# Two transformer layers on one core: the first group normalised by VectorE, casts dealt out over the groups, and a gather of two rows ahead of the indices

## The reference

```python
xn = _layernorm(x, axis=-1)                      # no scale, no bias, eps 1e-5
x = x + L0_attn(xn, Wq, Wk, Wv, Wo) + L0_ffn(xn, Wg, bg, W1, b1, W2, b2)
xn = _layernorm(x, axis=-1)
x = x + L1_attn(xn, w_qkv, w_proj, b_proj) + L1_ffn(xn, W_r, W_k, W_v, mu_r, mu_k)
# L0_attn: q, k, v = xn @ W.T, 16 heads of 8; rotary turn of q and k; phi = elu + 1;
#          causal linear attention: running sums of k and of k (x) v, num / den; @ Wo.T
# L0_ffn:  gate = softmax(xn @ Wg + bg) over 8 experts, top 2, weights made to sum to 1;
#          each expert: gelu(xn @ W1[e] + b1[e]) @ W2[e] + b2[e]
# L1_attn: the same kind of attention without causality; L1_ffn: r * (relu(k)^2 @ W_v)
```

## Time and profile before

| | |
|---|---|
| median of the runs | 356.3 us |
| the profiled execution | 356.63 us, its span 354.8 us |
| granted TensorE clock over the span | 0.995 |
| busy: TensorE, VectorE, ScalarE, GpSimd | 340.7, 318.8, 272.5, 210.4 us |
| front (to the start of the choice) | 0 to 35.8 us |
| choice, turns, tables | 35.8 to 59.6 us |
| first expert matmul | 64.23 us |
| last gather's transpose | 264.3 us |

### The profile page before, as it was taken

The page is one execution under the profiler, slowest core; times in us unless marked ns, Lnnn a source line. Parts: engine busy times, 40 slices in busy tenths (PEclk is TensorE's granted clock), DMA queues, the critical chain, the costliest instruction groups (busy, mean ns, idle before and its releaser), DMA issues.

```text
span 354.8 us, 9147 instructions
## 1 busy us (share of the span) xinstructions
PE 340.7 (96%) x2498; PEld 297.2 (84%) x2498; DVE 318.8 (90%) x629; ACT 272.5 (77%) x767; POOL 210.4 (59%) x231
## 2 busy tenths in 40 slices
PE   8999968999999999999999999999999899999995
PEld 3788524699999999999999899999998687778885
DVE  3998899799999999999899899998987799998665
ACT  3887957966988888888687878778985987777751
POOL 3899201853343666766676768777877268884110
PEclk9999989999999999999999999999999999999999
DMA  6866295345353545554555644565452002221112
GB/s 190 237 187 188 82 427 188 107 143 140 98 164 113 173 140 161 148 165 128 178 153 147 172 148 145 158 174 150 132 136 76 17 7 54 60 62 30 30 31 59
DMA packets 45520, 46.98 MB, mean 132 GB/s; under 512 B 6928, under 2 KB 33712, under 8 KB 45216
## 3 DMA queue, kind: packets, MB, share of 16 engines
q1 hardware_dynamic: 40288, 36.88, 33.8%
q0 software_dynamic: 4320, 8.86, 9.5%
q10 hardware_dynamic: 864, 0.67, 0.7%
HBM read 32.88 MB, written 13.50 MB: 131 GB/s over the span
## 4 chain that ended last, share of the span: by engine, by line
PE 86%; DVE 7%; ACT 2%; DMA 2%; issue 2%; POOL 0%; DVEq 0%; POOLq 0%
PE banks L546 18%; PE banks L533 18%; PE banks L672 7%; PE banks L673 7%; PE banks L984 3%; PE banks L342 3%; PE banks L311 3%; PE banks L517 3%; PE banks L1013 2%; PE banks L1060 2%; PE banks L1042 2%; PE banks L333 2%; PE banks L1022 2%; PE banks L748 2%; PE banks L994 2%
## 5 line engine op out<-in xcount | busy, mean ns | idle before, releaser
L461 POOL DMA_INDIRECT xg<-xn_rows,slot_tok x71 | 77.9, 1098 | 77.6 <-PE banks L517 41.6
L563 ACT ACTIVATE xT<-banks,b1T 128x128 f32<-128x128 f32 x284 | 81.7, 375 | 18.1 <-PE banks L533 17.8
L478 POOL DMA_INDIRECT qk_exp<-expert_rows,ranki x64 | 74.1, 1158 | 19.1 <-issue 18.8
L546 PE MATMUL banks<-w_sb,xT 128*128 x568 | 79.0, 282 | 0.0
L533 PE MATMUL banks<-xgT,w 128*128 128x128 f32 x568 | 75.4, 276 | 0.1
L546 PEld LDWEIGHTS banks<-w_sb,xT 128*128 128x128 f32 x568 | 69.3, 192 | 0.6
L533 PEld LDWEIGHTS banks<-xgT,w 128*128 128x128 f32 x568 | 69.0, 192 | 0.6 <-issue 0.6
L684 DVE TENSOR_TENSOR cq<-banks,phi 128x360 f32<-128x360 f32 (+1 forms) x96 | 47.3, 548 | 7.1 <-PE banks L673 6.4
L656 DVE TENSOR_TENSOR low<-outer,high 128x1152 fp32r<-128x1152 f32 x32 | 43.5, 1358 | 4.5 <-ACT high L650 4.3
L650 ACT CAST high<-outer 128x1152 fp32r<-128x1152 f32 x32 | 36.9, 1154 | 9.9 <-DVE outer L639 8.6
L693 DVE TENSOR_REDUCE sums<-cq 128x144 f32<-128x1152 f32 x32 | 43.0, 1342 | 0.1
(11 more groups left out here) (206 smaller groups left out, 687.8 us busy)
## 6 DMA issues: line engine op xcount, KB each, us to landing
w<-in_L_ffn_W SPq DMA_DIRECT2D x71, 256.0 KB
expert_rows<-ye SPq DMA_DIRECT2D x71, 64.0 KB
expert_rows<-x_sb SPq DMA_DIRECT2D x2, 2048.0 KB, 9.0
x_sb<-in_L_attn_x SPq DMA_DIRECT2D x8, 256.0 KB, 4.0
xn_rows<-xn SPq DMA_DIRECT2D x8, 256.0 KB, 2.4
w_sb<-in_L_ffn_W SPq DMA_DIRECT2D x8, 256.0 KB, 3.2
out<-outer SPq DMA_DIRECT2D x7, 256.0 KB, 2.4
xg<-xn_rows,slot_tok POOLq DMA_INDIRECT x71
```

What stands on the lines that cost most here:

```text
L461: pool.indirect_dma_start(out=xg[n][:, :], out_offset=None, in_=xn_dram, in_offset=bass.IndirectOffsetOnAxis(ap=slot_tok[:, j:j + 1], axis ...
L478: pool.indirect_dma_start(out=y_moe[:, i, k, :], out_offset=None, in_=y_dram, in_offset=bass.IndirectOffsetOnAxis(ap=ranki[:, 0, k, i:i + ...
L546: last = nc.tensor.matmul(y, hidT[p][:, c, :], w2_sb[:, ds(e * NC + c, 1), :], start=False, stop=(c == NC - 1))
L563: last = nc.scalar.activation(hidT[p][:, c, :], slot_bank(j)[:, c * P:(c + 1) * P], ACT.Gelu_apprx_tanh, bias=b1T[:, ds(e * NC + c, 1)])
```

## The change

VectorE normalises group 0 itself from mean and rstd (`normalise_first`), tile by tile; GpSimd leaves out the last two operations of `deviation` for that group. TensorE transposes group 0 in two halves into two banks (`xT_first`), ScalarE copies them half by half (`xT_first_scalar`), and TensorE starts the values with the first half (`values1_half`). Nearly all warming matmuls around this go. Queries and keys rotate over three banks (4, 5, 3) instead of two, and a half waits for the products three halves back; the counts of the ranks move from bank 3 to bank 1. The load of the second part of the constants moves from ScalarE's queue to SP's, behind x of group 4; the seven casts go to groups 1 to 4, two, two, two and one. The flags of two memsets are merged. On GpSimd a gather of two rows into `y_tok`, which nobody reads, stands between a wait for `turn_key` and a wait for its own landing, ahead of the wait for `idx_ready`.

```diff
     def deviation(pool, layer, g, n):
...
         nc.gpsimd.tensor_tensor(rstd[n][:, :], ve[n][:, :], mhalf[:, :], ALU.pow).then_inc(rstd_part[layer], 1)
+        if layer == 0 and g == 0:
+            return
...
+    def normalise_first(v):
+        v.wait_ge(rstd_part[0], 1)
+        for k in range(GT):
+            nc.vector.tensor_scalar(xn[0][:, k, :], x_sb[:, k, :], mv[0][:, k, 0:1], rstd[0][:, k:k + 1],
+                                    ALU.subtract, ALU.mult).then_inc(xn_ready[0], 1)
...
+    def xT_first(pe):
+        for h in range(2):
+            for t in range(2):
+                pe.wait_ge(xn_ready[0], 2 * h + t + 1)
+                last = nc.tensor.transpose(ps[h][:, t * P:(t + 1) * P], xn[0][:, 2 * h + t, :], ident)
+            last.then_inc(xT_ps, 1)
+            keep_warm(1)
...
+    def qk_bank(g, h):
+        return ps[(4, 5, 3)[(2 * g + h) % 3]]
 
     def queries1_tensor(pe, g, h, p):
-        if g:
-            pe.wait_ge(rope_ready, g * 2 + h - 1)
+        if g * 2 + h >= 3:
+            pe.wait_ge(rope_ready, g * 2 + h - 2)
...
+    def xT_first_scalar(act):
+        for h in range(2):
+            act.wait_ge(xT_ps, h + 1)
+            nc.scalar.copy(xT[0][:, 2 * h:2 * h + 2, :].rearrange("p a b -> p (a b)"), ps[h][:, 0:2 * P]
+                           ).then_inc(xT_ready, 1)
...
-    counts = ps[3][:, 0:NPRE]
+    counts = ps[1][:, 0:NPRE]
...
             sp.wait_ge(wts_in, 16 * 4)
-            for g in range(2, NG):
+            for g in range(2, 5):
+                load_x(g)
+            sp.dma_start(cq[:, 0:NCONST - NKEPT], consts[:, NKEPT:]).then_inc(passing_in, 16)
+            for g in range(5, NG):
                 load_x(g)
...
-            act.dma_start(cq[:, 0:NCONST - NKEPT], consts[:, NKEPT:]).then_inc(passing_in, 16)
...
-            normalise(act, 0, 0)
-            xT_scalar(act, 0, 0)
+            xT_first_scalar(act)
             normalise(act, 0, 1)
             for g in range(NG):
                 for h in range(2):
                     values1_scalar(act, g, h)
+                if g == 1:
+                    act.wait_ge(passing_in, 16)
+                    # 2 casts; 2 more at g == 2, 2 at g == 3, 1 at g == 4 (all 7 stood behind g == 0)
...
             for n in range(NB):
                 pool.wait_ge(xn_saved[n], 16 * (NG // NB))
+            pool.wait_ge(turn_key, 1)
+            pool.indirect_dma_start(out=y_tok[0:2, 0:D], out_offset=None, in_=xn_dram,
+                                    in_offset=bass.IndirectOffsetOnAxis(ap=ranki[0:2, 1, 0, 0:1], axis=0)
+                                    ).then_inc(first_rows, 16)
+            pool.wait_ge(first_rows, 16)
             pool.wait_ge(idx_ready, 1)
...
-            keep_warm(3)
+            keep_warm(2)
+            xT_first(pe)
             pe.wait_ge(wT_ready, 1)
-            keep_warm(7)
-            xT_tensor(pe, 0, 0)
-            keep_warm(4)
             for g in range(NG):
-                values1_tensor(pe, g, g % 2)
-                queries1_tensor(pe, g, 0, g % 2)
+                if g:
+                    values1_tensor(pe, g, g % 2)
+                    queries1_tensor(pe, g, 0, g % 2)
+                else:
+                    values1_half(pe, 0, 0, 0)
+                    queries1_tensor(pe, 0, 0, 0)
+                    values1_half(pe, 0, 1, 0)
...
-            for g in range(5):
+            for g in range(2):
+                loaded_moments(g)
+            normalise_first(v)
+            for g in range(2, 5):
                 loaded_moments(g)
```

More of the change, by code:

```diff
@@ L294, in normalise @@
         n = g % NB
-        act.wait_ge(rstd_ready[layer], g + 1)
+        act.wait_ge(rstd_ready[layer], g + layer)
         if g >= NB:
             if layer == 0:
-                act.wait_ge(xT_ps, g - NB + 1)
+                act.wait_ge(xT_ps, g - NB + 2)
                 act.wait_ge(xn_saved[n], g // NB * 16)
@@ L312, in keep_warm @@
                              start=True, stop=True)
+    def xT_first(pe):
[5 more added lines that the diff above has]
+            keep_warm(1)
     def xT_tensor(pe, g, p):
-        pe.wait_ge(xn_ready[0], g + 1)
-        if from_(g, 2):
-            pe.wait_ge(xT_ready, g - 1)
+        pe.wait_ge(xn_ready[0], g + GT)
+        pe.wait_ge(xT_ready, max(g, 2))
         for k in range(GT):
@@ L326, in values1_tensor, with values1_half @@
     def values1_tensor(pe, g, p):
-        pe.wait_ge(xT_ready, g + 1)
         for h in range(2):
-            if g:
[L331 to L335, removed]
+            values1_half(pe, g, h, p)
+    def values1_half(pe, g, h, p):
+        pe.wait_ge(xT_ready, g + 2 if g else h + 1)
+        if g:
+            pe.wait_ge(v_raw, g * 2 + h - 1)
+        for t in range(2):
+            last = nc.tensor.matmul(ps[6 + h][:, t * NV:(t + 1) * NV], xT[p][:, 2 * h + t, :], w_in[:, 2 * D:NQ],
+                                    start=True, stop=True)
+        last.then_inc(v_ps, 1)
+    def qk_bank(g, h):
+        return ps[(4, 5, 3)[(2 * g + h) % 3]]
     def queries1_tensor(pe, g, h, p):
-        if g:
-            pe.wait_ge(rope_ready, g * 2 + h - 1)
+        if g * 2 + h >= 3:
+            pe.wait_ge(rope_ready, g * 2 + h - 2)
         for t in range(2):
-            last = nc.tensor.matmul(ps[4 + h][:, t * 2 * D:(t + 1) * 2 * D], xT[p][:, 2 * h + t, :], w_in[:, 0:2 * D],
+            last = nc.tensor.matmul(qk_bank(g, h)[:, t * 2 * D:(t + 1) * 2 * D], xT[p][:, 2 * h + t, :], w_in[:, 0:2 * D],
                                     start=True, stop=True)
         last.then_inc(qk_ps, 1)
+    def xT_first_scalar(act):
[3 more added lines that the diff above has]
+                           ).then_inc(xT_ready, 1)
     def xT_scalar(act, g, p):
-        act.wait_ge(xT_ps, g + 1)
+        act.wait_ge(xT_ps, g + 2)
         if from_(g, 2):
@@ L1269, in _ @@
             sp.wait_ge(bias_split, 5)
-            sp.wait_ge(bias_zero, 1)
+            sp.wait_ge(zeros_ready, 2)
             for n in range(3):
@@ L1326, in _ @@
                     values1_scalar(act, g, h)
+                if g == 1:
+                    act.wait_ge(passing_in, 16)
+                    nc.scalar.copy(ones_bf[:, :], passing("ones"))
+                    nc.scalar.copy(tri_bf[:, :], passing("tri_excl"))
+                if g == 2:
+                    nc.scalar.copy(tri_r[:, :], passing("tri_incl"))
+                    nc.scalar.copy(ones_r[:, :], passing("ones"))
+                if g == 3:
+                    nc.scalar.copy(token[:, :, :].rearrange("p g n -> p (g n)"), passing("token"))
+                    nc.scalar.copy(row_mat[:, :], const("row_no").broadcast_to([P, P]))
+                if g == 4:
+                    nc.scalar.copy(row_no2[:, :, :], passing("iota").unsqueeze(2).broadcast_to([P, P, 2])
+                                   ).then_inc(small_ready, 1)
                 if g + 1 < NG:
@@ L1330, in _ @@
                     normalise(act, 0, g + 2)
[L1331 to L1340, removed]
             exp_relu(act, 0)
@@ L1466, in _ @@
             pe.wait_ge(w_late_in, 16 * 5)
-            pe.wait_ge(xT_ready, NG)
+            pe.wait_ge(xT_ready, NG + 1)
             for n in range(4):
@@ L1619, in _ @@
             done(position(pos_hi, 1))
-            v.wait_ge(xT_ready, NG)
+            v.wait_ge(xT_ready, NG + 1)
             v.wait_ge(qk_ps, NG * 2)
```

12 lines of the change are left out of this document (7 added, 5 removed).

## The result

| | before | after |
|---|---|---|
| median (22 runs each, same chip) | 356.31 us | 354.79 us |
| ratio, with its 95% interval | | 0.9962 [0.9951, 0.9973] |
| profiled execution, its span | 356.63, 354.8 us | 354.96, 353.1 us |
| the choice starts (first VectorE operation) | 35.77 | 33.38: 2.39 early |
| scan of the choice starts | 42.47 | 40.78: 1.69 early |

Faster, by 0.38%: 1.5 us between the medians, 1.7 between the spans. The prediction had 2.3. The table shows where to look: the front gave 2.4, and 0.7 of it was gone 7 us later. From there on, all is shifted alike.

The account below looks back on a forecast made before the run. TensorE, holding 86% of the chain of waits, was taken as the bound, nearly gapless from 64 us. Front 2.2 plus gather 0.1 gave 2.3 us: 354.0 against the median, own range 353.5 to 354.5, wide range 352.4 to 355.3.

Parts of the forecast that it names:

- rival (a): Front, group 0: VectorE's new normalising blocked by GpSimd through shared ports, tiles up to 1.0 us late; 354.7, chance 0.15.
- Front: From start to choice of experts: earlier first values move the choice forward; -2.2 us, bounds -1.6 and -2.7.
- VectorE late next: Front: after five groups' moments, ending near 12.5, VectorE owes products and three moments until 33.2 us.
- the choosing starts 2.1 early: End of the front: last values at 32.0 instead of 34.10, so the choice of experts starts at 33.65.
- no cost, but no reserve: Front: nearly full GpSimd, order unchanged, reaches the shifts of groups 6 and 7 about when ScalarE asks; nothing lost.
- Gather: Before the first expert slot: the extra two-row gather gains 0.1 us, bounds -0.6 and +2.
- being first costs 0.6 us: First real gather starts 0.90 after slot_tok, a later one 0.27 after its transpose; the extra gather can absorb the difference.
- Casts: ScalarE in the front: dealt out 2, 2, 2, 1, they remove group 2's stall, costing 0 to 0.1 us each.
- Constants' queue: Front: moving the constants' load to SP's queue may land x of group 2 earlier; 0.1 us taken.
- Rival (b): At the turns: TensorE's clock fall comes at another time or not at all, 1.3 us more gained; 352.7, chance 0.12.
- Rival (c): Front: with warming gone TensorE's clock falls before 9 us, adding 3.5 us; 357.5, chance 0.06.
- Rival (d): GpSimd full, so the expert rows' fill starts no earlier and meets first weights and gathers; 355.8, chance 0.11.

Follow-up runs that it names:

- neither move: Changed kernel with GpSimd's two sums of group 5 put on VectorE (0.9970, 355.63 us at 0.995), or later on GpSimd (0.9963, 355.12).
- merged without the gather: Changed kernel with GpSimd's small operations for groups 3 and 4 done once, no two-row gather, ten warming matmuls instead of thirteen: 0.9986 [0.9952, 1.0019].

## Why the prediction was right, and where it was off

The direction and the place were right; the size was 0.8 too large, and the time, 354.79, lies in the wide range (352.4 to 355.3) but outside the forecast's own (353.5 to 354.5). That it is so near rival (a)'s 354.7 is luck: the price is the same, but it was paid somewhere else.

- **Front, -2.2 predicted, -2.4 measured at the choice.** First values at 8.65 predicted, 8.71 measured; group 1 at 12.3 and 12.04, group 4 at 22.0 and 21.88, group 7 at 32.0 and 31.70. VectorE late next, with the moments ending near 12.5 (measured 12.56); TensorE meeting rope_ready late about group 4, measured twice, 0.3 to 0.4 each. The third bank as what makes the early start usable: shown by the run with two.
- **The failed step is the one after it:** "the choosing starts 2.1 early" was carried on to the end one for one, and GpSimd, "nearly full" and "with its order unchanged", was put down as "no cost, but no reserve". Its shifts did come in time. But its sums end when they ended before, and the choice moved under them. The cost is 0.73 and 0.51 on the two operations, less the 0.53 by which the scan now follows closer on the operation ahead of it (0.60 from start to start, 1.13 before, when it waited for TensorE): 0.7, shown by leaving the sums out of either kernel. A sign of it stood in the earlier trace rows: L1550 took 0.55, with GpSimd at work until 36.04; without the sums it took 0.42.
- **Gather, -0.1 predicted, 0 measured.** That the exponential hides it was right. That "being first costs 0.6 us", and that the extra gather can take this on itself, was wrong: it took 0.1.
- **Casts.** The prediction counts on the stall at group 2 going when they are dealt out. It went, and with the casts together it is back (0.67, the values of group 2 start 0.96 later). But VectorE's backlog takes most of that: 0.35 is left at the choice and nothing at the scan.
- **Constants' queue.** 0.1 predicted, nothing measured.
- **Rival (a)** was not seen where it was placed: four tiles in 1.11 beside GpSimd's 1.01 at 7.38, nowhere a microsecond late (0.28 a tile; the prediction took 0.2 and bounded it at 0.25). Its rule was at work elsewhere. The runs show VectorE held beside GpSimd's adds of 512 columns: operations with two inputs 0.42 to 0.93 and up to 1.57, and a tensor_scalar 0.17 to 0.54. In the changed kernel the second one ended 0.29 after the last sum. This agrees with the Trainium skill, SBUF — State Buffer, Who interferes with whom: a VectorE instruction with two inputs in SBUF contends with a GpSimd instruction that reads SBUF, and the one that comes second is blocked for the whole of the other. The excess, 1.15 at most, is never more than one sum's 1.27. Its price, 0.7, is the one that rival (a) had; the prediction looked for the rule only beside the new operations and not beside those that the change pushed into GpSimd's work.
- **Rival (b).** The clock fell in the profile as before (0.50 in 47.00:50.00). Its price was wrong: no fall is worth 0.4 to 0.5 at slot_tok, not 1.3 (last section).
- **Rival (c)** did not come: the granted clock is 1.00 in every stretch until 43.95. **Rival (d)**'s first half, the gain handed back because GpSimd is full, is what happened, but through VectorE's operations and not through the fill.

## What to carry to other kernels

When a change pulls a serial stretch forward, list what the engines with unchanged schedules do at its new place: work that ended just before it now lies beside it, and here a VectorE operation with two inputs took two to nearly four times as long beside GpSimd's adds (0.93 to 1.57 instead of 0.42). An odd duration in the trace of before (0.55 where the same shape takes 0.42) is the warning, and leaving the suspected neighbour out of both kernels prices it. Where GpSimd is the full engine, doing fewer of its small operations may be worth more than another move of its large ones: here that brought the key forward by 0.8, and neither move brought it forward at all.

## What was not expected

- The run times of one kernel fall in levels by the granted clock over the span: after, 354.37 at 1.0, 354.75 at 0.995 and 356.12 at 0.99 (5, 10 and 7 runs). The profiles show a place, the turns: from the key to slot_tok it takes 10.44 where the clock stays at 1.00 (two banks, and merged without the gather), 10.85 to 10.98 with the usual fall (ten profiles, both kernels among them) and 12.0 where the fall lasts longer (without the gather, and with the constants on ScalarE's queue). The last is seen in this window of the changed kernel without the gather, where the changed kernel's profile is back at 1.00 from 50 us on:
```profile
51.00:53.00 2.00, 2.00 (x6) 0.73 (x5) 1.26 (x7) 1.08 (x4) 0.00 (x0) 0.52 1.03 442
```
  There the second six matmuls of zeros take 2.46 in the chain of waits instead of 1.40, and the tables' matmuls stand behind them. What decides between the three in one and the same kernel stays open.
- The gather of two rows took 6.7 us to land beside the fill of the expert rows, where the first real one took 2.8 with 64 times the rows. In the other kernels it took 4.2 to 6.8.
